# Transposing the MLP's activations and x3 on DVE instead of PE, and moving the mix and LoRA-down B in PE's order

## The reference

```
x = x + S4D(x)                   # causal convolution along the 512 steps, masked by a length per item
x = x + einsum('bct,bcd->bdt', x, W1[cond[b]])
x = x + einsum('bct,bcd->bdt', x, W2[cond[b]])
x = x + MLP(x)                   # 512 -> 1376 -> 512 along the last axis, a LoRA entry per item
gate = x Wg' + 0.5 Bg[i] (Ag[i] x);  up = x Wu' + 0.5 Bu[i] (Au[i] x)
act = silu(gate) * up;  down = act Wd' + 0.5 Bd[i] (Ad[i] act)
```

## Time and profile before

| | us |
|---|---|
| median of 3 runs (lowest, highest) | 1070.89 (1070.21, 1073.7) |
| the profiled execution, and its span | 1069.72, 1067.9 |
| busy: PE, DVE, ACT, POOL | 1037.9 (97%), 490.4 (46%), 402.1 (38%), 484.8 (45%) |

### The profile page before, as it was taken

One profiled execution on the slowest core, in us unless ns is written; L12 is line 12 of the kernel. 1 busy time (PEld: TensorE's weight loads), 2 busy tenths in 40 slices (PEclk: granted clock), 3 DMA queues, 4 the chain that ended last, 5 costly groups with the idle time before them and its releaser, 6 DMA issues.

```text
span 1067.9 us, 19023 instructions
## 1 busy us (share of the span) xinstructions
PE 1037.9 (97%) x5922; PEld 906.3 (85%) x5922; DVE 490.4 (46%) x1095; ACT 402.1 (38%) x627; POOL 484.8 (45%) x301
## 2 busy tenths in 40 slices
PE   3999899999999999999999999999999999999998
PEld 3665688888898888888888988888888888888887
DVE  8333344545444445445454445454454444454442
ACT  7002234434433433344343334334443433443341
POOL 0605354545445444545454454445454544544441
PEclk9999899999999999999999999999999999999999
DMA  9799342424333343424243333434242433334320
GB/s 340 249 404 337 116 110 89 134 69 138 98 109 101 99 123 101 120 84 136 71 138 97 108 99 101 125 99 122 80 137 73 137 96 107 102 98 128 104 75 20
DMA packets 100980, 135.50 MB, mean 127 GB/s; under 512 B 26395, under 2 KB 59420, under 8 KB 100956
## 3 DMA queue, kind: packets, MB, share of 16 engines
q1 hardware_dynamic: 100380, 135.12, 41.3%
q10 hardware_dynamic: 576, 0.08, 0.1%
HBM read 118.11 MB, written 16.99 MB: 127 GB/s over the span
## 4 chain that ended last, share of the span: by engine, by line
PE 94%; DVE 3%; DMA 3%; issue 0%; ACT 0%; DVEq 0%; ACTq 0%
PE ps L984 47%; PE ps L1016 27%; PE ps L994 8%; PE ps L962 5%; PE ps L1005 4%; DMA x1p<-yo 2%; PE ps L1039 1%; PE ps L1038 1%; PE ps L975 1%; PE ps L972 1%; PE ps L973 1%; DVE x3r L815 0%; DMA tr<-kpad 0%; DVE xs L704 0%; PE ps L936 0%; PE ps L1027 0%
## 5 line engine op out<-in xcount | busy, mean ns | idle before, releaser
L984 PE MATMUL ps<-wg_hi,x_hi 128*128 128x512 f32 (+2 forms) x768 | 299.2, 390 | 4.6 <-DVE x_lo L805 4.6
L984 PE MATMUL ps<-wg_lo,x_hi 128*128 128x512 f32 (+2 forms) x768 | 291.7, 380 | 0.0
L984 PE MATMUL ps<-wg_hi,x_lo 128*128 128x512 f32 (+2 forms) x768 | 290.7, 379 | 0.0
L471 POOL TENSOR_TENSOR bst<-braw,bst 128x1024 fp32r<-128x1024 f32 (+1 forms) x96 | 212.7, 2215 | 90.7 <-ACT bst L572 90.7
L815 DVE STREAM_TRANSPOSE x3r<-x3n 32x128 f32<-32x128 f32 x512 | 155.0, 303 | 92.3 <-ACT x3n L545 85.8
L588 ACT ACTIVATE at_hi<-ps 128x512 fp32r<-128x512 f32 (+1 forms) x95 | 53.4, 562 | 315.1 <-PE ps L1005 315.1
L984 PEld LDWEIGHTS ps<-wg_hi,x_hi 128*128 128x128 f32 x768 | 145.1, 189 | 25.9 <-issue 4.7
L984 PEld LDWEIGHTS ps<-wg_hi,x_lo 128*128 128x128 f32 x768 | 145.1, 189 | 25.2
L984 PEld LDWEIGHTS ps<-wg_lo,x_hi 128*128 128x128 f32 x768 | 145.3, 189 | 20.4
L1016 PE MATMUL ps<-wd_hi,at_hi 128*128 128x288 f32 x696 | 151.9, 300 | 0.0
L1016 PE MATMUL ps<-wd_lo,at_hi 128*128 128x288 f32 x696 | 149.0, 296 | 0.0
(11 more groups left out here) (147 smaller groups left out, 1184.6 us busy)
## 6 DMA issues: line engine op xcount, KB each, us to landing
braw<-in_tb SPq DMA_DIRECT2D x256, 128.0 KB, 2.7
braw<-in_tb SPq DMA_DIRECT2D x128, 96.0 KB, 2.4
adraw<-in_tad SPq DMA_DIRECT2D x128, 88.0 KB, 1.9
tr<-kpad SPq DMA_DIRECT2D x16, 512.0 KB, 6.9
x1p<-yo SPq DMA_DIRECT2D x16, 512.0 KB, 5.7
xb<-in_x SPq DMA_DIRECT2D x32, 256.0 KB, 2.8
agraw<-in_ta SPq DMA_DIRECT2D x128, 64.0 KB, 2.0
bdraw<-in_tbd SPq DMA_DIRECT2D x128, 64.0 KB, 2.2
```

The source lines that it names most:

```text
L471: sub(v, b_from(p, q), v.bitcast(F32), ALU.subtract).then_inc(s["blo"], 1)
L984: last = mm(bank[:, 0:n], x3s[a][:, k, :], wgs[b][:, k, o:o + n], start=(k == 0 and a + b == 0), stop=False, skip_group_check=True)
```

## The change

PE no longer transposes activations in the loop (the last part of the last tile excepted). DVE does it in 16 blocks of 32 partitions for each part, from `act_t` into the bank `atp` (`a_turn`, on a new semaphore `atv`). x3 is copied to a new buffer `x3m`, turned from there into its own bank `misc` in two pieces (3 blocks, then 13), and ACT copies `x3m` to `x3n` later (`x3_keep`, semaphore `x3k`). On PE, `mix(t + 1)` moves from behind `chunk(p, 2, 0)` to behind `lora_b(t, p, 0)`; `down(t - 1, ..., 2)` follows it; `chunk(p, 1, 0)` moves ahead of `lora_b(t, p, 0)`, and `lora_b_down` behind `lora_b(t, p, 1)`. `x1_high` and `x1_low`, which the mix needs, move forward on ACT and POOL.

```diff
@@ -167,7 +167,7 @@
         x3s = [sb("x3_hi", [P, KT, TN], F32R), sb("x3_lo", [P, KT, TN], F32R)]
-        x3r = sb("x3r", [P, T])
+        x3m = sb("x3m", [P, T])
         act_t = sb("act_t", [P, T])
@@ -481,10 +481,10 @@
                     x_sum(t + 1)
+                    x1_low(t + 1)
                 b_low(t, p, 1)
...
                     ag_low(t + 1)
-                    x1_low(t + 1)
                 b_low(t, p, 2)
@@ -540,15 +540,21 @@
 
-            def x3_copy(t, p):
+            def x3_copy(t):
                 act.wait_ge(s["x3mm"], t + 1)
-                copy(x3n[:, p, :], misc, ACT.Copy).then_inc(s["x3n"], 1)
+                copy(x3m[:], misc, ACT.Copy).then_inc(s["x3n"], 1)
+
+            def x3_keep(t, p, free=None):
+                act.wait_ge(s["x3n"], t + 1)
+                if free is not None:
+                    act.wait_ge(s["evac"], free)
+                copy(x3n[:, p, :], x3m[:], ACT.Copy).then_inc(s["x3k"], 1)
 
...
                     act.wait_ge(s["gu"], free)
-                copy(x3s[0][:].rearrange("p k n -> p (k n)"), x3r[:], ACT.Copy).then_inc(s["x3hi"], 1)
+                copy(x3s[0][:].rearrange("p k n -> p (k n)"), misc, ACT.Copy).then_inc(s["x3hi"], 1)
 
@@ -584,7 +590,14 @@
                 n = PAIRS[q][1] - PAIRS[q][0]
-                act.wait_ge(s["att"], t * 3 + q + 1)
+                if to is not None:
+                    act.wait_ge(s["att"], 1)
+                else:
+                    if q == 0:
+                        act.wait_ge(s["td"], t)
+                    else:
+                        act.wait_ge(s["dn"], t * 2 + q)
+                    act.wait_ge(s["atv"], t * 3 + q + 1)
                 copy((ats[0] if to is None else to)[:, 0:n * P], atp[:, 0:n * P], ACT.Copy).then_inc(s["ahi"], 1)
@@ -601,8 +614,9 @@
             act.wait_ge(s["yst1"], 16 * C // 4)
-            x3_copy(0, 0)
+            x3_copy(0)
             x3_high(0)
+            x3_keep(0, 0)
             act.wait_ge(s["msk"], 1)
@@ -611,23 +625,25 @@
                 t_high(t)
+                if not last:
+                    x1_high(t + 1)
                 b_high(t, p, 1, None if first else t * 3)
                 silu(t, p, 0)
+                if not last:
+                    x3_copy(t + 1)
+                    ag_high(t + 1)
+                a_high(t, 0)
                 if not first:
                     td_high(t - 1)
-                a_high(t, 0)
-                if not last:
-                    ag_high(t + 1)
-                    x1_high(t + 1)
                 b_high(t, p, 2, t * 3 + 1)
...
                 if not last:
-                    x3_copy(t + 1, 1 - p)
-                a_high(t, 1)
-                if not last:
+                    x3_keep(t + 1, 1 - p, None if first else t)
                     ad_high(t + 1, 1 - p, None if first else t)
                     b_high(t + 1, 1 - p, 0, t * 3 + 2)
+                a_high(t, 1)
+                if not last:
                     x3_high(t + 1, t * 3 + 3)
@@ -802,18 +818,29 @@
                 dve.wait_ge(s["x3hi"], t + 1)
-                tt(x3s[1][:].rearrange("p k n -> p (k n)"), x3r[:], x3s[0][:].rearrange("p k n -> p (k n)").bitcast(F32),
+                tt(x3s[1][:].rearrange("p k n -> p (k n)"), misc, x3s[0][:].rearrange("p k n -> p (k n)").bitcast(F32),
                    ALU.subtract).then_inc(s["x3lo"], 1)
 
-            def x3_turn(t, p):
-
+            def turn(to, of, blocks, tail=False):
+
+                for i, j in blocks:
+                    n = KT if not tail else FT % KT - (j * C >= FTAIL)
+                    rows, cols = slice(i * C, (i + 1) * C), slice(j * C, (j + 1) * C)
+                    last = V.transpose(to[cols].rearrange("f (k n) -> f k n", n=P)[:, 0:n, rows],
+                                       of[rows].rearrange("n (k f) -> n k f", f=P)[:, 0:n, cols])
+                return last
+
+            GRID = [(i, j) for i in range(GB) for j in range(GB)]
+
+            def x3_turn(t, part, done=False):
                 dve.wait_ge(s["x3n"], t + 1)
-                for i in range(GB):
-                    for j in range(GB):
-                        part = x3n[i * C:(i + 1) * C, p, :].rearrange("n (k f) -> n k f", f=P)[:, :, j * C:(j + 1) * C]
-                        turned = x3r[j * C:(j + 1) * C, :].rearrange("f (k n) -> f k n", n=P)[:, :, i * C:(i + 1) * C]
-                        last = V.transpose(turned, part)
-                last.then_inc(s["x3t"], 1)
+                last = turn(misc, x3m[:], part)
+                if done:
+                    last.then_inc(s["x3t"], 1)
+
+            def a_turn(t, q):
+                dve.wait_ge(s["mul"], t * 3 + q + 1)
+                turn(atp, act_t[:], GRID, q == 0).then_inc(s["atv"], 1)
 
@@ -861,6 +888,7 @@
                 dve.wait_ge(s["accd"], t + 1)
+                dve.wait_ge(s["x3k"], t + 1)
                 if stored is not None:
@@ -873,29 +901,34 @@
             tt(x1_lo[:], xa[:], x1_hi[:].bitcast(F32), ALU.subtract).then_inc(s["x1lo"], 1)
-            x3_turn(0, 0)
+            x3_turn(0, GRID, True)
             x3_low(0)
...
                     act_mul(t - 1, 1 - p, 2)
+                    a_turn(t - 1, 2)
                 t_mask(t, p)
...
                 t_low(t)
+                act_mul(t, p, 0)
+                a_turn(t, 0)
                 if not first:
...
                     td_turn(t - 1)
-                act_mul(t, p, 0)
+                if not last:
+                    x3_turn(t + 1, GRID[0:3])
                 if not first:
...
                 a_low(t, 0)
+                if not last:
+                    x3_turn(t + 1, GRID[3:16], True)
                 if not first:
...
                 act_mul(t, p, 1)
-                if not last:
-                    x3_turn(t + 1, 1 - p)
+                a_turn(t, 1)
                 a_low(t, 1)
@@ -1015,8 +1048,8 @@
                                       start=(q == 0 and j == j0 and a + b == 0), stop=False, skip_group_check=True)
-                if q == 2:
-                    last.then_inc(s["td"], 1)
+                if blocks is None:
+                    last.then_inc(s["td" if q == 2 else "dn"], 1)
 
@@ -1050,29 +1083,28 @@
                 chunk(p, 0, 0).then_inc(s["la"], 1)
-                if not first:
-                    a_turn(t - 1, 2)
                 chunk(p, 0, 1)
                 if not first:
-                    down(t - 1, 1 - p, 2)
+                    pe.wait_ge(s["mul"], t * 3)
+                chunk(p, 1, 0)
                 pe.wait_ge(s["tlo2"], t + 1)
                 lora_b(t, p, 0)
-                chunk(p, 1, 0)
-                a_turn(t, 0)
+                if not last:
+                    mix(t + 1, 1 - p)
+                if not first:
+                    down(t - 1, 1 - p, 2)
                 chunk(p, 1, 1)
+                lora_b(t, p, 1)
                 if not first:
                     lora_b_down(t - 1, 1 - p)
-                lora_b(t, p, 1)
+                pe.wait_ge(s["mul"], t * 3 + 1)
                 chunk(p, 2, 0)
...
                     pe.wait_ge(s["wlo"], 9)
-                if not last:
-                    mix(t + 1, 1 - p)
                 pe.wait_ge(s["adlo"], t + 1)
                 down(t, p, 0)
-                a_turn(t, 1)
                 chunk(p, 2, 1)
```

More of the change, by code:

```diff
@@ L185, in cond_resid_kernel @@
             ag aghi aglo ad adhi adlo b0 b1 bhi blo bd bdhi bdlo
-            bfree la tm tmt thi2 tlo2 gu silu mul att ahi alo td tdm tdt tdhi tdlo accd evac ost""".split() + [
+            bfree la tm tmt thi2 tlo2 x3k gu silu mul att atv dn ahi alo td tdm tdt tdhi tdlo accd evac ost""".split() + [
             f"wl{n}" for n in range(NW)] + [f"u{q}" for q in range(C // 2)]
@@ L625, in tile_act @@
                 if not last:
-                    x3_copy(t + 1, 1 - p)
+                    x3_keep(t + 1, 1 - p, None if first else t)
+                    ad_high(t + 1, 1 - p, None if first else t)
+                    b_high(t + 1, 1 - p, 0, t * 3 + 2)
                 a_high(t, 1)
                 if not last:
-                    ad_high(t + 1, 1 - p, None if first else t)
-                    b_high(t + 1, 1 - p, 0, t * 3 + 2)
                     x3_high(t + 1, t * 3 + 3)
```

## The result

The changed kernel took 1288.19 us (median of 4 runs, 1286.88 to 1291.08) where the kernel before took 1070.55 on the same chip: a ratio of 1.2031, 95% interval 1.1998 to 1.2065. It is 20% slower. The forecast was 1270 in a range of 1215 to 1320, with slower at 0.96.

What follows compares the result with a forecast made beforehand. PE bounded the kernel before; afterwards a cycle through DVE, SP's queue and the mix, 69.4 us a block plus 2.8 for the clock. Fourteen blocks of 72.2 with start and end gave 1274, less 4: 1270, range 1215 to 1320.

Steps and rivals of the forecast that it cites:

- Step 1: PE in the tile loop: losing its transposes saves at most 1.20 us per tile, 38 us in all.
- Step 2: DVE's queue: 14.5 us more transposes per tile, 0.316 us each; DVE alone makes a tile 31.2 us.
- Step 3: Mix in a block's first tile waits about 9 us for `wbd` behind SP's queue; block 69.4 us against 58.83.
- Step 4: PE's clock falls to half speed after each block's long mix wait: 2.8 us lost, 72.2 per block.
- Step 5: Whole run: fourteen blocks of 72.2 us plus start and end give 1274, less 4 for PSUM writes: 1270.
- (a): Rival on PE's clock: it stays up or comes back at once, 45 us less, 1227; chance 0.17.
- (b): Rival on DVE: a transpose into PSUM costs 0.38 us, 4.2 us more per block, 1333; chance 0.10.
- (c): Rival at the mix: `wbd` is there in time, only DVE's queue counts, 31.2 per tile, 1130; chance 0.08.
- (d): Rival on PE, the faster side: its 1.20 us per tile come back whole, 1033; chance 0.03.

Runs made afterwards that it cites:

- the new kernel: Kernel before, with DVE transposing parts 0 and 2, PE keeping part 1, x3 into PSUM and part 2's transposes all ahead of `t_mask`: 1040.60 us, 0.9719.
- the kernel with SP's order turned: Changed kernel, but SP issues the DMAs of `wbd` ahead of the tile's other loads (part 2's LoRA B, LoRA A, LoRA-down A): 1189.58 us, 1.1128.
- the experiment: Changed kernel, but PE runs 64 idle matmuls before the mix in each block's first tile (the very first excepted): 1257.40 us, 1.1758.
- Each half: Moves alone (changed kernel, PE transposing activations again): 1270.37 us. Transposes alone (kernel before, all three activation groups on DVE): 1272.93 us.

## Why the prediction was right

**Step 1, the most the change can give (38 us).** Held as far as it was tried. Two of the three groups on DVE, with no new wait, gave 29 us. By this step's price they are worth 0.44 + 0.32 us a tile, 24 us. The rest fits a short wait of the kernel before that went too: from the last LoRA B of part 2 to `down(t,1)` it took 1.06 us (615.53 to 616.59), in the new kernel 0.93 (629.60 to 630.53), and `down` itself 3.28 and 3.20, 0.2 us a tile or some 6 in all.

**Step 2, DVE's work.** The transposes are 323 ns, 287 and 264 by their width, 16 of them 5.36 us, a pace of 0.335 where I took 0.316. It lies inside the bounds of 0.285 and 0.38, but on the dearer side, and I had taken 4 us off because a single row, which was no transpose, seemed to point below 0.316. 64 on a block's path at 0.019 more are 1.2 us.

**Step 3, the mix waits for `wbd`, by way of SP.** Held in its size. From the mix to `down(t,1)` 20.9 us (18.3 and 2.8 for the clock were forecast), from there to `outb` 24.6 (23.9), from `outb` to the next block's mix 27.4 (27.2). PE waits 8.4 to 8.6 us there (9 forecast) and 1.0 in the block's second tile (1.4). SP waits 11.1 us on the mean at `store_out` (9 to 12), DVE is busy for 70% (75). The waits before `down` are a little longer than the 1 us allowed: 1.03 to 1.06 for `at_lo`, 0.6 to 1.3 for the accumulators. That SP's queue, and no engine, is what the long wait hangs on is shown by the kernel with SP's order turned.

**Step 4, the clock.** 1.9 and 2.9 us after the two waits shown, 2.1 on the mean by the experiment; 2.8 forecast.

**Step 5, the sum.** The mix of tile 2 came at 203.9 (204 forecast), that of tile 30 at 1226.2 (1211.5): 73.3 a block (72.2 forecast; the first took 75.2, the others 72.4 to 73.8, the last less), 14 x 1.1 = 15. The end took 1.1 more, the 4 us taken off were wrong, and what lies outside the span was 1.6 less: 15 + 1 + 4 - 2 = 18, the whole of what was missed. The term that was mis-sized is the transpose into PSUM.

**The rivals.** (a), a clock that stays up: false; it fell in every block, and by the experiment would have given some 31 us, where I priced it at 45. (b), a transpose at 0.38: the sign is right, a third of the size. The Trainium skill's 60 ns of overhead on SBUF and 125 on PSUM (Perfetto Trace Analysis, "Optimizing Scalar/DVE Operations") doesn't hold for this operation: 23 ns between the two, and the measurement decides. (c), `wbd` in time: false here, and true of the kernel with SP's order turned, which took 1190 where I had worked out 1130 for DVE alone. In its trace the tiles take 33.4, 34.3, 31.0 and 34.3 us in turns, and only the one of 31.0 is what I had worked out. In the other three DVE stands idle for 3.5 to 5.3 us at part 0's multiplication (2.4 in the short one). PE waits 0.7 to 1.05 us for `wbd` at every second mix, and in two of the four the clock has fallen behind the wait before `down(t, 0)`, where DVE stands 1.2 us more before `x3_low`. The worked-out time for DVE alone had none of this; how the 60 us divide among these isn't shown. (d), faster: false.

What the prediction didn't see is that the change is slow twice over. It treated the transposes as 14.5 us more on a path that the moves had made. Each half is enough for a loss of 200 us.

## What to carry to other kernels

When work goes from the bound engine to one with 54% of its time free, the share says nothing; what counts is each consumer that was just in time, and each instruction that now stands ahead of its producer in that queue. Draw the whole cycle, the DMA queue and the order of its issues in it as well, before an instruction is moved towards its producer. And if a variant gives only a part of what it should, look on the receiving engine for an instruction that waits while ready work stands behind it: one such place here, mended together with ACT's order, brought 26 of 29 us.

## What the hardware showed that I had not expected

**Two inputs in SBUF beside GpSimd.** DVE's subtraction for x3 takes 2.13 us before the change and 0.69 where it reads PSUM, with the same operation of GpSimd beside it. First DVE and GpSimd in the kernel before, then in the one with x3 in PSUM alone; last the first x3 of the kernel before, when GpSimd did nothing until 121.07:

```profile
617.32 2.13 DVE L805 TENSOR_TENSOR x_lo<-x3r,x_hi 128x512 fp32r<-128x512 f32 x1 [0.79 <-ACT x_hi L551]
```

```profile
617.06 1.84 POOL L471 TENSOR_TENSOR bst<-braw,bst 128x768 fp32r<-128x768 f32 x1
```

```profile
624.60 0.69 DVE L804 TENSOR_TENSOR x_lo<-ps,x_hi 128x512 fp32r<-128x512 f32 x1 [0.43 <-ACT x_hi L550]
```

```profile
624.37 1.84 POOL L470 TENSOR_TENSOR bst<-braw,bst 128x768 fp32r<-128x768 f32 x1
```

```profile
120.20 0.69 DVE L805 TENSOR_TENSOR x_lo<-x3r,x_hi 128x512 fp32r<-128x512 f32 x1 [0.69 <-ACT x_hi L551]
```

The slow one ends at 619.45, that is 0.55 us after GpSimd's operation. With both inputs in SBUF and no GpSimd beside it the same operation takes 0.69, so it is the two together that cost. The Trainium skill (SBUF — State Buffer, "SBUF: two separate sides") has the rule: a DVE operation with two SBUF inputs and a GpSimd operation that reads SBUF hold one port pair in turns, each for its whole length. The rows agree with it, but for the 0.14 us by which 0.55 is shorter than 0.69.

**The clock's way back.** After a wait of 8.5 us the granted clock was at 1.00 again some 4 to 6 us behind PE's first matmul (from 648.5 in the first block shown, from 723.5 in the second). Waits of 0.65 to 1.25 us left it at 1.00 (652 to 700 us in the changed kernel). With SP's order turned, it fell to 0.50 behind 15 of 30 waits of 2.1 us. And a block transpose costs 300 ns to SBUF and 323 to PSUM at 128 columns.
